# Making the scores of two attention steps together in a fused attention and mixture-of-experts kernel

## The chip, the cores and the metric

One NeuronCore of a Trainium2 chip runs the whole kernel. The metric is the device time of one execution in microseconds (us). Nothing runs on the other cores.

## The reference

The input is x (4 batches, 2048 tokens, 256 features, float32). The reference is one transformer layer, with a layer norm behind each half:

```python
Q = sign(x * sign(bv_q)); K = sign(x * sign(bv_k)); V = x * sign(bv_v)
scores = einsum('btd,bsd->bts', Q, K) * d ** -0.5
attn = where(causal, sigmoid(scores * 4.0), 0.0)
x = layernorm(x + einsum('bts,bsd->btd', attn, V))

# top-1 mixture of 32 experts, capacity 320 rows each
probs = softmax(x @ w_router); top1 = argmax(probs)
y = (silu(buf @ w_gate) * (buf @ w_up)) @ w_down   # per expert
out = layernorm(x + where(accepted, y[slot] * gate, 0.0))
```

The attention has no softmax: each weight is a sigmoid of its own score, so a block of weights can be used as soon as its scores exist.

## The kernel before

The kernel is written with an instruction stream for each engine by hand; semaphores order them. Five engines work: TensorE (PE), VectorE (DVE), ScalarE (ACT), GpSimd (POOL), and SyncE (SP), which only issues DMAs. Each engine runs its own stream in order.

**Attention steps.** A batch has four groups of 512 queries (g = 0 to 3). Group g needs 4g + 4 blocks of 128 keys, so a batch has 4 + 8 + 12 + 16 = 40 steps (`NS`), numbered k = 0 to 39; the groups begin at k = 0, 4, 12 and 24. There are four batches, 160 steps in all. A step goes through three engines:

- `scores(b, k)` on PE: two bfloat16 matmuls (line 899) of 128 keys by up to 512 queries into one of four PSUM banks (`SB = 4`, bank k % 4). The last four steps of a group lie on the diagonal: they have 512, 384, 256 and 128 queries, and one small matmul more for the mask (line 896).
- `weights(b, k)` on ACT: two sigmoids of the same scores, one rounded into `hl_ring` (line 694), one in full back into the bank (line 696).
- `low(b, k)` on DVE: their difference, the low part of the weight (line 1173). It frees the bank.
- `values(b, k)` on PE: for each tile of 128 queries three matmuls of 256 columns (lines 921 to 923), so 12 in a full step and 12, 9, 6 and 3 on the diagonal. They add up in PSUM over the steps of the group.

`scores` of step n waits until `low` of step n - 4 has freed the bank (semaphore `al_ready`). `values(b, k)` waits for `low(b, k)` too. PE's order in every step k from 2 on is: the scores of step k + 4, then the values of step k.

**Work between the steps.** Behind the values of chosen steps PE does work for the groups that are finished: `turn_x1` (8 transposes, line 940), `router` (16 matmuls of 32 output rows, line 953), `turn_logits` (line 959) and `counts` (5 small bfloat16 matmuls, lines 966 to 971). The steps are written out in tables; a key is the group, and group 3 is done in the batch that follows:

```python
TURN = {3: 5, 0: 11, 1: 20, 2: 29}
ROUTE = {3: 6, 0: 12, 1: 24, 2: 30}
LTURN = {3: 6, 0: 13, 1: 26, 2: 31}
COUNT = {3: 8, 0: 17, 1: 28, 2: 34}
NORM = {3: (6, 6, 7, 7), 0: (10, 11, 11, 11), 1: (21, 22, 23, 23), 2: (30, 31, 31, 32)}   # ACT
COPY = {3: 9, 0: 14, 1: 23, 2: 33}     # ACT
LCOPY = {3: 9, 0: 16, 1: 28, 2: 34}    # ACT
```

ACT's tables count ACT's own steps: `normalise` (line 704) stands behind `weights` of the steps in `NORM`, `copy_x1t` (two copies, line 711) behind `weights` of the step in `COPY`, and so on. `turn_x1` waits for the four normalised tiles, the copies wait for `turn_x1`, each half of `router` waits for one of the two copies, `copy_lgt` (line 716) waits for `router`, and `turn_logits` waits for `copy_lgt`. ACT is thus several steps ahead of PE in step numbers: the copies that PE's step 6 waits for stand behind `weights` of step 9, and those that its step 30 waits for behind `weights` of step 33.

DVE adds the residual from PSUM at the end of a group (line 1180), takes statistics, and makes the routing decisions. SP waits at line 347 for a count of `scores_ready` before it transposes the signs of the next batch by DMA (line 348).

After the attention comes the expert part (from about 313 us): `gate_up` (lines 1077 to 1085) and `down` (lines 1100 to 1111). The change doesn't touch it.

Of the kernel before, what the change touches and what calls it, by code (L numbers as in the profile page):

```python
# [34 lines left out]
SB = 4  # L35
# [28 lines left out]
def bass_postln_attn_moe_kernel(nc, x, bv_q, bv_k, bv_v, w_router, w_gate, w_up, w_down, out):  # L64
# [16 lines left out]
    NS = len(STEPS)  # L81
# [8 lines left out]
    with ExitStack() as ctx:  # L90
# [168 lines left out]
        def atleast(eng, s, value, settle=False):  # L259

            if isinstance(value, int) and value <= 0:
                return
            if settle and not isinstance(value, int):
                value = eng.to_reg(value)
                eng.wait_ge(consts, 11)
            eng.wait_ge(s, value)
# [43 lines left out]
        def cols(k):  # L312

            g, j = STEPS[k]
            return g, j, max(0, j - GT * g) * P
# [553 lines left out]
        def _(pe):  # L869
# [8 lines left out]
            def scores(b, k):  # L878

                g, j, lo = cols(k)  # L880
                n = b * NS + k
                if j == 0:
                    if b == 0:
                        pe.wait_ge(qt_ready, g + 1)
                    else:
                        pe.wait_ge(qt_in, 16 * ((b - 1) * NG + g + 1))
                if j == GT * g:
                    if n == 0:
                        pe.wait_ge(key_first, 1)
                    pe.wait_ge(kt_ready, DC * (b * NG + g + 1) - 1)  # L890
                atleast(pe, al_ready, n - SB + 1)
                o = ps[:, k % SB, lo:GQ]
                diag = j >= GT * g
                if diag:

                    mm(ps[:, k % SB, lo:lo + P], identb[:, :], maskb[:, :], start=True, stop=False,
                       skip_group_check=True)
                for c in range(DC):
                    last = mm(o, k_t[:, c, j * P:(j + 1) * P], q_t[:, g, c, lo:GQ],  # L899
                              start=(c == 0 and not diag), stop=(c == DC - 1), skip_group_check=diag)  # L900
                last.then_inc(scores_ready, 1)

            def values(b, k):

                g, j, lo = cols(k)
                n = b * NS + k
                r = k % WRING
                if n == 0:
                    pe.wait_ge(v_first, 1)
                elif n == 1 or j == GT * g:  # L910
                    pe.wait_ge(v_ready, b * NG + g + 1)
                pe.wait_ge(ah_ready, n + 1)
                pe.wait_ge(al_ready, n + 1)
                for i in range(lo // P, GT):
                    if j == 0 and i % 2 == 0:

                        atleast(pe, res_ready, (b * NG + g - 1) * GT + i + 2)
                    o = ps[:, PV + i // 2, (i % 2) * D:(i % 2 + 1) * D]
                    ah = hl_ring[:, 0, r, i * P:(i + 1) * P]
                    al = hl_ring[:, 1, r, i * P:(i + 1) * P]  # L920
                    mm(o, ah, v_hl[:, 0, j, :], start=(j == 0 and i % 2 == 0), stop=False, skip_group_check=True)  # L921
                    mm(o, ah, v_hl[:, 1, j, :], start=False, stop=False, skip_group_check=True)  # L922
                    last = mm(o, al, v_hl[:, 0, j, :], start=False, stop=(j == GT * g + i), skip_group_check=True)  # L923
                last.then_inc(pv_done, 1)

            def turn_signs(b, q):
                n = b * NG + q
                pe.wait_ge(sgn_ready, n + 1)
                o = ps[:, M1, :].bitcast(BF16).rearrange("p (c t) -> p c t", c=DC)
                for c in range(DC):  # L930
                    for i in range(GT):
                        last = nc.tensor.transpose(o[:, c, i * P:(i + 1) * P], sgn[:, c, i, :],
                                                   identb[:, :])
                last.then_inc(sgn_turned, 1)

            def turn_x1(G, par):
                for i in range(GT):
                    pe.wait_ge(x1_ready, G * GT + i + 1)
                    for c in range(DC):
                        last = nc.tensor.transpose(ps[:, M0 + c, i * P:(i + 1) * P],  # L940
                                                   xrow[:, par, i, c * P:(c + 1) * P], ident[:, :])
                last.then_inc(x1_turned, 1)

            def router(G):
                if G == 0:
                    pe.wait_ge(w_r_in, 16)
                for c in range(DC):
                    if G == B * NG - 1 and c == 1:
                        pe.wait_ge(x1t_late, 1)
                    else:  # L950
                        pe.wait_ge(x1t_ready, DC * G + c + 1)
                    for i in range(GT):
                        last = mm(ps[i * E:(i + 1) * E, M0, 0:P], w_r[:, c, :], x1_t[:, c, i * P:(i + 1) * P],  # L953
                                  start=(c == 0), stop=(c == DC - 1))
                last.then_inc(lgt_done, 1)

            def turn_logits(G):
                pe.wait_ge(lgt_ready, G + 1)
                nc.tensor.transpose(ps[:, M0, 0:GT * E], lg_t[:, :], ident[:, :]).then_inc(logits_done, 1)

            def counts(G):

                pe.wait_ge(hot_ready, G + 1)
                pe.wait_ge(seen_ready, G + 1)
                rows = hot[:, G % 2, :, :]
                mm(logits, tri[:, :], rows[:, 0:GT, :], start=True, stop=False, skip_group_check=True)
                for h in range(GT - 1):
                    mm(logits[:, h + 1:GT, :], onesb[:, :],
                       rows[:, h, :].unsqueeze(1).broadcast_to([P, GT - 1 - h, E]), start=False, stop=False,
                       skip_group_check=True)  # L970
                mm(logits, onesb[:, :], rows[:, GT, :].unsqueeze(1).broadcast_to([P, GT, E]), start=False, stop=True,
                   skip_group_check=True).then_inc(counts_done, 1)

            def batch(b, first, last):
                for k in range(NS):
                    if first and k < 2:
                        values(0, k)
                        if k == 0:
                            turn_signs(0, 1)
                        else:  # L980
                            scores(0, SB)
                            scores(0, SB + 1)
                    else:
                        if k + SB < NS:
                            scores(b, k + SB)
                        elif not last:
                            scores(b + 1, k + SB - NS)
                        values(b, k)
                    for g in (3, 0, 1, 2):
                        if g == 3 and first:  # L990
                            continue
                        G = (b - 1 if g == 3 else b) * NG + g
                        if k == TURN[g]:


                            prepared = NG if b > 0 else 2 + sum(PREP[q] < k for q in (2, 3))
                            atleast(pe, slot_ready, G)
                            pe.wait_ge(qt_ready, prepared)
                            turn_x1(G, g % 2)
                        if k == ROUTE[g]:  # L1000
                            router(G)
                        if k == LTURN[g]:
                            turn_logits(G)
                        if k == COUNT[g]:
                            counts(G)
                    for q in range(NG):
                        if first and k == PREP[q] and q not in AHEAD:
                            pe.wait_ge(qt_ready, q)
                            turn_signs(0, q)
# [5 lines left out]
            for k in range(SB):  # L1015
                scores(0, k)
            keep_warm(5, bank=M0)
            batch(0, True, False)
            for b in range(1, B - 1):
                batch(b, False, False)  # L1020
            batch(B - 1, False, True)
            G = B * NG - 1
            pe.wait_ge(al_ready, B * NS)
# [475 lines left out]
```

## Time and profile before

| what | value |
|---|---|
| median of 3 runs | 538.89 us (538.89 to 539.34) |
| profiled execution | 538.01 us |
| its span, first to last instruction | 536.3 us |
| PE busy | 515.2 us, 96% of the span |
| DVE, ACT, POOL busy | 406.3, 380.8, 384.6 us |
| attention steps on PE | to 301 us |

The span is what the trace shows; the 1.7 us between it and the time of the profiled execution lie ahead of the first and behind the last instruction. Matmuls are pipelined, so their busy times overlap: a matmul's row shows its start and how long it was in the array, and two that follow each other without a gap start less than one duration apart. What a group of matmuls costs is read as the distance between the end of the row ahead of it and its own end.

### The profile page before, as it was taken

What the parts mean: (1) busy time and instruction counts of PE and PEld (TensorE: products, weight loads), DVE (VectorE), ACT (ScalarE), POOL (GpSimd) and SP (SyncE); (2) the same over time, 40 slices, a digit from 0 to 9 for tenths busy, and PEclk for the clock granted to TensorE, in tenths of its full rate; (3) what the DMA queues carried; (4) which work ended last, traced back from release to release, by engine and by line L of the source; (5) the groups of instructions that cost most, each with busy time, mean ns of one, the idle gap of its engine ahead of it and who ended that gap; (6) DMA issues with size and microseconds to landing.
All of it is one profiled execution on the core that took longest, in us unless ns stands there. A gap on an engine that the chain in (4) does not pass through costs nothing.

```text
span 536.3 us, 12197 instructions
## 1 busy us (share of the span) xinstructions
PE 515.2 (96%) x4028; PEld 457.9 (85%) x4028; DVE 406.3 (76%) x1026; ACT 380.8 (71%) x775; POOL 384.6 (72%) x497
## 2 busy tenths in 40 slices
PE   6999999999999999999999999999999999999992
PEld 5889899898998898998989648999889999999981
DVE  3785787876777948788766636888888888888873
ACT  5885969769878869788686414777677677776762
POOL 4547877777879678777785270578877878787876
PEclk9999999999999999999999999999999999999997
DMA  7995332263332533328841016487776667786211
GB/s 247 371 355 195 90 99 61 79 178 101 110 85 81 108 117 87 95 46 275 247 156 62 1 49 153 125 252 208 224 207 193 199 202 213 216 241 184 76 41 51
DMA packets 91903, 81.54 MB, mean 152 GB/s; under 512 B 31626, under 2 KB 83066, under 8 KB 91840
## 3 DMA queue, kind: packets, MB, share of 16 engines
q1 hardware_dynamic: 84848, 66.39, 42.5%
q0 software_dynamic: 6912, 14.30, 7.9%
q8 instruction: 33, 0.54, 0.4%
q14 instruction: 30, 0.25, 0.2%
q10 hardware_dynamic: 80, 0.07, 0.0%
HBM read 44.33 MB, written 37.90 MB: 153 GB/s over the span
## 4 chain that ended last, share of the span: by engine, by line
PE 91%; POOL 2%; issue 2%; DVE 2%; DMA 2%; ACT 1%; SPq 0%; ACTq 0%; POOLq 0%; DVEq 0%
PE ps L921 12%; PE ps L922 12%; PE ps L923 12%; PE ps L899 11%; PE ps L1077 8%; PE ps L1085 7%; PE ps L1078 7%; PE ps L1103 5%; PE ps L1111 3%; PE ps L1050 3%; PE ps L940 2%; PE ps L953 2%; PE ps L1100 1%; PE ps L1102 1%; PE ps L1101 1%
## 5 line engine op out<-in xcount | busy, mean ns | idle before, releaser
L921 PE MATMUL ps<-v_hl,hl_ring 128*128 128x256 f32 x544 | 178.6, 328 | 0.3 <-DVE hl_ring L1173 0.3
L922 PE MATMUL ps<-v_hl,hl_ring 128*128 128x256 f32 x544 | 153.6, 282 | 0.0
L923 PE MATMUL ps<-v_hl,hl_ring 128*128 128x256 f32 x544 | 153.3, 282 | 0.0
L921 PEld LDWEIGHTS ps<-v_hl,hl_ring 128*128 128x128 f32 x544 | 103.5, 190 | 15.1 <-issue 0.7
L1173 DVE TENSOR_TENSOR hl_ring<-ps,hl_ring 128x512 fp32r<-128x512 f32 (+3 forms) x160 | 94.1, 602 | 19.0 <-ACT ps L696 14.0
L922 PEld LDWEIGHTS ps<-v_hl,hl_ring 128*128 128x128 f32 x544 | 103.8, 191 | 2.7
L923 PEld LDWEIGHTS ps<-v_hl,hl_ring 128*128 128x128 f32 x544 | 103.4, 190 | 0.0
L694 ACT ACTIVATE hl_ring<-ps 128x512 fp32r<-128x512 f32 (+3 forms) x160 | 86.3, 539 | 22.2 <-PE ps L899 21.9
L696 ACT ACTIVATE ps<-ps 128x512 f32<-128x512 f32 (+3 forms) x160 | 87.4, 546 | 0.0
L536 POOL DMA_INDIRECT expert_rows<-xrow,slot x64 | 64.3, 1005 | 29.0 <-issue 22.8
L899 PE MATMUL ps<-q_t,k_t 128*128 128x512 bf16 (+3 forms) x320 | 85.1, 350 | 0.0
L1077 PE MATMUL ps<-hl_ring,v_hl 128*128 128x320 f32 x256 | 80.8, 328 | 0.3 <-DVE hl_ring L1441 0.3
L1078 PE MATMUL ps<-hl_ring,v_hl 128*128 128x320 f32 x256 | 76.0, 309 | 0.0
L620 POOL DMA_INDIRECT out_dram<-alone,ids x55 | 56.9, 1035 | 16.6 <-issue 14.4
L1077 PEld LDWEIGHTS ps<-hl_ring,v_hl 128*128 128x128 f32 x256 | 48.1, 188 | 7.0 <-issue 6.5
L1279 DVE TENSOR_TENSOR v_hl<-xall,v_hl 128x1280 fp32r<-128x1280 f32 x32 | 47.8, 1497 | 7.1 <-issue 7.1
L816 ACT ACTIVATE a_buf<-ps 128x320 f32<-128x320 f32 x64 | 28.0, 437 | 34.0 <-PE ps L1085 34.0
L1078 PEld LDWEIGHTS ps<-hl_ring,v_hl 128*128 128x128 f32 x256 | 48.2, 188 | 0.4
L1085 PE MATMUL ps<-hl_ring,v_hl 128*128 128x320 f32 x256 | 48.0, 310 | 0.0
L489 POOL TENSOR_TENSOR v_hl<-z,v_hl 128x1024 fp32r<-128x1024 f32 x15 | 36.0, 2402 | 12.7 <-ACT v_hl L686 12.7
L732 ACT ACTIVATE v_hl<-xall 128x1280 fp32r<-128x1280 f32 x32 | 40.5, 1266 | 1.6 <-PE ps L923 1.6
L834 ACT ACTIVATE alone<-z,zrs 128x256 f32<-128x256 f32 x54 | 29.0, 594 | 17.7 <-POOL zrs L607 16.3
(163 smaller groups left out, 1127.0 us busy)
## 6 DMA issues: line engine op xcount, KB each, us to landing
expert_rows<-xs SPq DMA_DIRECT2D x40, 258.0 KB, 6.2
xs<-expert_rows SPq DMA_DIRECT2D x32, 258.0 KB, 2.8
xall<-in_L_attn_x_dram SPq DMA_DIRECT2D x16, 512.0 KB, 5.1
out_dram<-alone SPq DMA_DIRECT2D x16, 512.0 KB, 3.5
xall<-in_L_ffn_w_gate_dram SPq DMA_DIRECT2D x32, 256.0 KB, 3.9
xall<-in_L_ffn_w_up_dram SPq DMA_DIRECT2D x32, 256.0 KB, 4.3
xall<-in_L_ffn_w_down_dram SPq DMA_DIRECT2D x32, 256.0 KB, 4.8
xs<-expert_rows SPq DMA_DIRECT2D x31, 64.5 KB, 3.1
```

The lines of the kernel that those rows point to most:

```text
L536: g_.indirect_dma_start(out=buf_rows, out_offset=bass.IndirectOffsetOnAxis(ap=slot[:, par, i:i + 1], axis=0), in_=xrow[:, par, i, :], in_o ...
L620: g_.indirect_dma_start(out=out_rows, out_offset=bass.IndirectOffsetOnAxis(ap=ids[:, e % NIDS, t:t + 1], axis=0), in_=o_s[e % 3][:, t, :], ...
L694: s_.activation(hl_ring[:, 0, k % WRING, lo:GQ], ps[:, k % SB, lo:GQ], ACT.Sigmoid, scale=0.25)\
L696: s_.activation(ps[:, k % SB, lo:GQ], ps[:, k % SB, lo:GQ], ACT.Sigmoid, scale=0.25)\
L899: last = mm(o, k_t[:, c, j * P:(j + 1) * P], q_t[:, g, c, lo:GQ], start=(c == 0 and not diag), stop=(c == DC - 1), skip_group_check=diag)
L921: mm(o, ah, v_hl[:, 0, j, :], start=(j == 0 and i % 2 == 0), stop=False, skip_group_check=True)
L922: mm(o, ah, v_hl[:, 1, j, :], start=False, stop=False, skip_group_check=True)
L923: last = mm(o, al, v_hl[:, 0, j, :], start=False, stop=(j == GT * g + i), skip_group_check=True)
L1077: mm(o, wh, xh[:, c, :], start=(c == 0), stop=False)
L1078: mm(o, wl, xh[:, c, :], start=False, stop=False)
L1085: last = mm(o, wh, xl[:, c, :], start=False, stop=(c == DC - 1))
L1173: v_.tensor_tensor(hl_ring[:, 1, r, lo:GQ], ps[:, k % SB, lo:GQ], hl_ring[:, 0, r, lo:GQ].bitcast(F32), ALU.subtract).then_inc(al_ready, 1)
```

## The change

In every even step PE makes the scores of steps k + 3 and k + 4, then the values of step k. In odd steps it makes only values. Step 1 of the first batch makes the scores of step 4 and leaves those of step 5 to step 2. No instruction is added or removed, and the other engines' streams are as they were. Since `NS` is even, the scores of even steps stay where they were (ahead of the values of the step four before), and those of odd steps go behind the values of the step four before, and behind whatever PE does after these values.

```diff
                         else:
                             scores(0, SB)
-                            scores(0, SB + 1)
                     else:
-                        if k + SB < NS:
-                            scores(b, k + SB)
-                        elif not last:
-                            scores(b + 1, k + SB - NS)
+
+                        for n in (k + SB - 1, k + SB) if k % 2 == 0 else ():
+                            if n < NS:
+                                scores(b, n)
+                            elif not last:
+                                scores(b + 1, n - NS)
                         values(b, k)
```

## Rows read from the trace of the kernel before

**Rows 1.** The page: busy times, and the clock granted to PE in 40 slices.

```profile
PE 515.2 (96%) x4028; PEld 457.9 (85%) x4028; DVE 406.3 (76%) x1026; ACT 380.8 (71%) x775; POOL 384.6 (72%) x497
...
PEclk9999999999999999999999999999999999999997
```

**Rows 2.** Busy times by stretch: PE, PEld, DVE, ACT, POOL, clock, DMA, GB/s.

```profile
13.00:301.00 288.00, 286.77 (x2472) 258.86 (x2472) 216.83 (x575) 227.80 (x484) 211.65 (x251) 1.00 0.47 140
```

**Rows 3.** Waits of PE and of its weight loads, 13 to 301 us, in full.

```profile
PE ps L959 <- ACT lg_t L716: 1.2, 3, 0.4
...
PEld ps L899 <- issue: 2.2, 11, 0.2
PEld ps L959 <- ACT lg_t L716: 2.0, 3, 0.7
PEld ps L921 <- ACT hl_ring L694: 0.3, 1, 0.3
PEld ps L921 <- DVE res L1180: 0.2, 1, 0.2
PEld ps L899 <- DVE hl_ring L1173: 0.2, 1, 0.2
```

**Rows 4.** PE's timeline around two score blocks: start, duration, instructions.

```profile
120.55 0.28 PE L923 MATMUL ps<-v_hl,hl_ring 128*128 128x256 f32 x1
120.67 0.61 PE L899 MATMUL ps<-q_t,k_t 128*128 128x512 bf16 x2
...
122.55 1.03 PE L940 MATMUL ps<-ident,xrow 128*128 128x128 f32 x8
123.42 0.59 PE L899 MATMUL ps<-q_t,k_t 128*128 128x512 bf16 x2
123.66 0.47 PE L921 MATMUL ps<-v_hl,hl_ring 128*128 128x256 f32 x1
```

**Rows 5.** The same timeline where 128-query scores stand ahead of values.

```profile
97.05 0.28 PE L899 MATMUL ps<-q_t,k_t 128*128 128x128 bf16 x2
97.14 0.37 PE L921 MATMUL ps<-v_hl,hl_ring 128*128 128x256 f32 x1
```

**Rows 6.** The same timeline behind a router.

```profile
142.21 0.65 PE L953 MATMUL ps<-x_t,w_r 128*32 128x128 f32 x16
142.79 0.60 PE L899 MATMUL ps<-q_t,k_t 128*128 128x512 bf16 x2
```

**Rows 7.** The same timeline in the expert part, half-width output ahead of full.

```profile
401.60 0.60 PE L1111 MATMUL ps<-xall,act_h 128*64 128x256 f32 x4
402.13 0.42 PE L1077 MATMUL ps<-hl_ring,v_hl 128*128 128x320 f32 x1
402.39 0.31 PE L1078 MATMUL ps<-hl_ring,v_hl 128*128 128x320 f32 x1
```

**Rows 8.** Groups of weight loads, 30 to 250 us: busy time, mean ns.

```profile
L922 PEld LDWEIGHTS ps<-v_hl,hl_ring 128*128 128x128 f32 x410 | 78.2, 191 | 2.1
...
L899 PEld LDWEIGHTS ps<-q_t,k_t 128*128 128x128 bf16 x242 | 17.2, 98 | 3.9 <-issue 1.8
```

**Rows 9.** Timelines of ACT and of PE, batch 1, steps 5 and 6 of PE.

```profile
93.02 0.48 ACT L694 ACTIVATE hl_ring<-ps 128x384 fp32r<-128x384 f32 x1
93.39 0.48 ACT L696 ACTIVATE ps<-ps 128x384 f32<-128x384 f32 x1
94.19 1.09 ACT L711 ACTIVATE x_t<-ps 128x512 f32<-128x512 f32 x2 [0.32 <-PE ps L940]
...
93.12 1.03 PE L940 MATMUL ps<-ident,xrow 128*128 128x128 f32 x8
95.79 0.64 PE L953 MATMUL ps<-x_t,w_r 128*32 128x128 f32 x16
```

**Rows 10.** Timelines of ACT and of PE, batch 1, steps 29 and 30 of PE.

```profile
138.15 0.60 ACT L694 ACTIVATE hl_ring<-ps 128x512 fp32r<-128x512 f32 x1
138.64 0.59 ACT L696 ACTIVATE ps<-ps 128x512 f32<-128x512 f32 x1
140.46 1.08 ACT L711 ACTIVATE x_t<-ps 128x512 f32<-128x512 f32 x2 [1.22 <-PE ps L940]
...
139.38 1.03 PE L940 MATMUL ps<-ident,xrow 128*128 128x128 f32 x8
```

**Rows 11.** Waits for scores: the SP queue's own, and ACT's from 30 to 250 us.

```profile
SPq L347 <- PE ps L899: 7.8, 3, 3.4
...
ACT hl_ring L694 <- PE ps L899: 16.7, 26, 1.2
```

## The prediction

> **What bounds the kernel now.** I read the page first, then the stretches, then PE's waits, then PE's timeline matmul by matmul. The page shows PE busy for 515.2 us of a span of 536.3 us, at full clock in all but the last slice [rows 1]. The stretch of the attention steps says it more sharply: from 13 to 301 us PE is busy 286.77 of 288 us, DVE 216.83, ACT 227.80 and POOL 211.65 us [rows 2]. A busy PE could still be one with slow matmuls, so the waits must be read as well: in these 288 us PE waits for another engine only at line 959 (3 times) and its weight loads three times more for 0.2 to 0.3 us [rows 3]. Nobody is late anywhere else. So the attention is as long as PE's stream of matmuls with the seams between them, and a change of PE's order can do two things only: change what the seams cost, or make another engine late where it is not late now. Behind 301 us nothing changes, and what PE loses or gains before then moves the end one for one.
>
> **The seams: how often each kind occurs.** PE's order follows from the loop and the four tables, so the seams can be counted by writing out the order of blocks for 4 x 40 steps, before and after. Each block of scores that follows values directly: 96 before, 55 after (41 fewer), because the second block of each pair now follows scores. Values behind 128-query scores: 15 before, 1 after (14 fewer), because the 128-query steps are odd (3, 11, 23, 39) and now have the next step's scores behind them. What comes instead: `router` stands in even steps, so behind 12 of the 15 routers now come values where scores came (the other three are followed by line 959 as before). `counts` is followed by values 11 times where it never was; `turn_x1` 4 times and `turn_logits` 7 times.
>
> **What each kind costs.** Costs are distances from end to end.
>
> - Scores behind values: from the end of line 923 at 120.83 to the end of both score matmuls at 121.28 is 0.45 us. Behind the transposes it is 123.58 to 124.01, 0.43 us [rows 4]. So the change from values to scores costs 0.02 us. 41 fewer: -0.8 us.
> - Values behind scores: the first value matmul ends 0.12 us after scores of 512 queries (124.01 to 124.13) [rows 4], the same as between value matmuls. Behind scores of 128 queries it is 97.33 to 97.51, 0.18 us [rows 5]; a row is only good to 0.01 us, and I take 0.05 us more than the ordinary 0.12. 14 fewer: -0.7 us. The reason is in the weight loads: that of a value matmul takes 191 ns, that of a score matmul 98 ns [rows 8], and behind a short matmul the long load shows.
> - Behind a router: the scores end 0.53 us after it (142.86 to 143.39) [rows 6] where 0.43 is ordinary, so 0.10 us are lost now. Values behind a router are nowhere in this trace. The bounds: at least 0.10 us as for scores, which would change nothing; the nearest row for more is in the expert part, where a full-width matmul with the same kind of 32-bit weights follows half-width ones: it ends 0.35 us after them (402.20 to 402.55), its successor 0.15 us later [rows 7], so 0.20 us lost. I take 0.20, since the load that can't be hidden there is of the long kind. 12 x (0.20 - 0.10) = +1.2 us; between 0 and +1.2.
> - Behind `counts`, whose last matmul is a short bfloat16 one like the 128-query scores: between 0 and 0.05 us by rows 5, I take 0.05. 11 times: +0.6 us.
> - Behind `turn_x1` and `turn_logits`: 11 times between 0 and 0.05 us. Their matmuls are longer, I take 0; at most +0.5 us.
>
> The seams together: -1.5 + 1.2 + 0.6 = +0.3 us, between -1.5 and +0.8 us.
>
> The Trainium skill ("TensorE: Matmul & The Clock Gate", section LDWEIGHTS) gives the weight load a time that depends on the number of columns alone. By that rule values behind a router would cost what scores do there, and the sum of the seams would be 1.2 us lower. The trace doesn't agree with it: for the same 128 columns it has 191 and 98 ns.
>
> **When the scores come, and who waits for them.** The scores of even steps stay in the same place of PE's work. Those of odd steps n are made behind the values of step n - 4 and not ahead of them, so they are up to 1.4 us later (12 x 0.12), and by the 1.03 us of `turn_x1` more where that stands in between (steps 5, 11 and 29, all odd). PE's own demand is unchanged: `low` of step k is needed at the same point of PE's work as before, by the scores ahead of `values(k)` or by these values themselves. And values of odd steps end one score block (0.43 us) earlier, which helps the residual adds that read them. The added lag is hidden as long as `weights` and `low` have that much to spare. That PE waited for `low` only once, 0.2 us, in 288 us [rows 3] says that they have some; ACT itself waits for scores 26 times between 30 and 250 us, 16.7 us in all [rows 11], so it mostly catches up at once. SP's wait for a count of scores ends up to 1.4 us later; it had waited 7.8 us in three places [rows 11]. Behind it stand the sign transpose and the next load of x, both for steps of the next batch, so this costs nothing.
>
> Two places have no such slack: the routers of group 3 (PE's step 6) and of group 2 (step 30), because the copies that they wait for stand on ACT behind `weights` of an odd step, 9 and 33, made just then.
>
> - Step 6, batch 1 [rows 9]. Before: `weights(9)` starts at 93.02 and ends at 93.87, the copies run from 94.19, and the router starts at 95.79. After: the values of step 5 end 0.40 us earlier (the three-tile scores of step 9 went), `turn_x1` ends at 94.15 - 0.40 = 93.75, the scores of step 9 at 94.13. `weights(9)` runs from 94.17 to 95.02; the copies, which overlap it by 0.1 us, end at 94.92 + 1.09 = 96.01. PE asks for the second copy about 0.13 us into the router, at 95.92 (an estimate: a fifth of its 0.64 us, since most of these are the emptying of its last matmuls). It waits 0.1 us. Three batches: 0.4 us.
> - Step 30 [rows 6, 10]. `turn_x1` ends at 140.41 - 0.45 = 139.96, the scores of step 33 at 140.41 (before, `weights(33)` had begun at 138.15), `weights(33)` runs to 140.45 + 1.08 = 141.53, the copies end at 141.43 + 1.08 = 142.51. PE asks for it at 142.21 + 0.13 = 142.34: it waits 0.2 us. Four batches: 0.8 us.
>
> Together +1.2 us. Below this, nothing, if the copies come a little sooner; above, each place may lose 0.5 us if ACT is also held by late normalisations: 3.5 us.
>
> **The sum.** +0.3 + 1.2 = +1.5 us on 538.01 us of the profiled execution: 539.5 us. The median of the runs lies 0.9 us above that execution, so I expect a median of 538.9 + 1.5 = 540.4 us.
>
> **Rivals.**
>
> 1. *No router waits, and values behind a router cost what scores do.* Then only the savings and the small costs stay: -1.5 + 0.6 = -0.9 us, 538.0 us; with nothing behind `counts` either, 537.4 us. For it: the waits that I found are 0.1 and 0.2 us, and rows 7 are of another stage. It is the one on the other side, and only with both conditions does it pass 0.2%. It decides if the second copy ends before PE is at the router's second half.
> 2. *ACT is late by more than one place.* The later scores of step 31 push its normalisations to where `turn_x1` of step 29 needs them, and `weights(33)` waits in turn. Each place then costs some 0.5 us: 7 x 0.5 - 1.5 + 1.8 = +3.8 us, 542.7 us. For it: four activations (two of weights, two of norms or copies, 0.5 us apart) are queued between. Against it: ACT is busy only 79% of the stretch.
> 3. *The seams cancel and the waits are half as large*: within 1 us of before, 539 to 539.9 us. All of the terms are small, so this is the neighbour of my forecast.
> 4. *Each seam costs far more than a row shows*, and halving their number is a real gain: 41 x 0.05 or so, -2 us, 536.9 us. Against it: rows 4 leave no room for it.
>
> **How the numbers follow.** My forecast (a loss between 1.1 and 3 us) has 0.41; rival 2 0.09; rival 3, with the weaker forms of rival 1, 0.38; rival 1 in full 0.08; rival 4 0.04. A difference of 0.2% (1.1 us) is about what a measurement of this kernel can tell from no change. That gives slower 0.50, the same 0.38, faster 0.12. The range goes from 538.0 us to 542.5 us; its ends come from rivals 1 and 2. The single number is 540.2 us, the sum rounded down a little because the largest seam term is an upper bound.
>
> **What the profile would show.** The lines of PE's waits should have new entries, line 953 waiting for line 711, seven times in the attention, 0.1 to 0.3 us each; line 959 should wait three times as before. In the timeline pairs of score blocks should end 0.86 us apart from the values ahead of them plus 0.02, and values behind a router 0.3 us behind it. `weights` of odd steps should start later, those of even steps mostly unchanged. The prediction is wrong if PE has waits at line 921 or 899 for line 1173 or 694 (then the lag was not hidden), if no wait at line 953 shows, or if values behind a router end only 0.2 us behind it.

## The result, and the profile after

| | before | changed |
|---|---|---|
| median | 538.89 us (6 runs) | 543.80 us (6 runs, 542.79 to 544.02) |
| profiled execution, span | 538.01, 536.3 us | 543.86, 541.4 us |
| ratio | | 1.0085, 95% interval 1.0075 to 1.0095 |

The changed kernel is slower: its median lies 4.9 us (0.9%) above that of the kernel before, and the measured ratio of the runs, which need not be the quotient of the two medians here and below, is 1.0085. I had forecast 540.2 us, slower, with a range to 542.5 us: the sign was right, the forecast loss of 1.3 us was about a quarter of what came, and the measured time lies outside my range. In the changed kernel and in those of the experiments the lines from the edit on are one to four further down: `low` is line 1174, the residual add 1181, the gate multiply 1247 (before: 1173, 1180 and 1246).

First the page of the changed kernel [rows 1 are its partners before].

```profile
PE 518.7 (96%) x4028; PEld 454.3 (84%) x4028; DVE 413.4 (76%) x1026; ACT 380.4 (70%) x775; POOL 384.1 (71%) x497
...
PEclk9999999999999999999999999999999999999996
```

PE's busy share is unchanged and says nothing: the clock is the same, and the waits are short. The stretches (columns as in [rows 2]) place the loss: with a boundary at 306 us in place of 301, the part behind it has the same 235 us, and PE is busy for 220.87 us of it where it was 220.75. The first row is of the kernel before, the other two of the changed one.

```profile
301.00:536.00 235.00, 220.75 (x1489) 192.71 (x1487) 184.79 (x444) 145.94 (x279) 167.41 (x223) 0.99 0.55 162
...
13.00:306.00 293.00, 290.09 (x2470) 255.17 (x2469) 223.75 (x575) 227.33 (x484) 211.07 (x251) 1.00 0.45 138
306.00:541.00 235.00, 220.87 (x1490) 192.73 (x1488) 184.93 (x444) 145.95 (x279) 167.45 (x223) 0.98 0.55 162
```

So the loss lies in the attention. PE's waits and those of its weight loads there, to be held against [rows 3]:

```profile
PE ps L921 <- DVE xs L1181: 1.7, 3, 0.6
PE ps L959 <- ACT lg_t L716: 1.2, 3, 0.4
...
PEld ps L921 <- issue: 2.8, 12, 0.3
PEld ps L921 <- DVE xs L1181: 2.3, 3, 0.8
PEld ps L959 <- ACT lg_t L716: 2.0, 3, 0.7
PEld ps L953 <- ACT x_t L711: 1.4, 7, 0.2
PEld ps L921 <- ACT hl_ring L694: 0.9, 4, 0.3
PEld ps L899 <- DVE hl_ring L1174: 0.9, 3, 0.3
PEld ps L940 <- ACT xrow L704: 0.3, 1, 0.3
```

Each row gives the total, the number of waits and the longest. The seven waits of the router for its copies are there as forecast. The largest entry is one that I had not thought of: three times a value matmul waits for the residual add. PE's timeline shows where (batch 1; the same in batches 2 and 3): inside the values of step 0.

```profile
84.32 0.71 PE L899 MATMUL ps<-q_t,k_t 128*128 128x128 bf16 x4
84.90 0.36 PE L921 MATMUL ps<-v_hl,hl_ring 128*128 128x256 f32 x1
...
85.57 0.28 PE L923 MATMUL ps<-v_hl,hl_ring 128*128 128x256 f32 x1
86.40 0.39 PE L921 MATMUL ps<-v_hl,hl_ring 128*128 128x256 f32 x1 [0.55 <-DVE xs L1181]
```

From the end of line 923 (85.85) to the end of the next line 921 (86.79) it is 0.94 us where 0.12 is ordinary: 0.82 us lost. The first value matmul of the step, at 84.90, also ends 0.23 us behind its scores, 0.11 more than ordinary; its weight load began at 84.87, 0.12 us after the first residual add had ended (84.75). Together 0.93 us, three times: 2.8 us, more than half of the loss.

The values of step 0 open a new group. They overwrite the PSUM banks that group 3 of the batch before has filled, so tiles 0 and 1 wait for the first residual add, and tiles 2 and 3 for the second, which DVE makes behind `low` of step 1. Why that add is late can be followed backwards through four engines. The same stations in the changed kernel (ACT, DVE, POOL, ACT, ACT, DVE):

```profile
76.14 0.49 ACT L694 ACTIVATE hl_ring<-ps 128x384 fp32r<-128x384 f32 x1 [1.27 <-PE ps L899]
...
77.11 0.56 DVE L1174 TENSOR_TENSOR hl_ring<-ps,hl_ring 128x384 fp32r<-128x384 f32 x1 [1.28 <-ACT hl_ring L694]
77.58 0.94 DVE L1245 RECIPROCAL quot<-sg 128x128 f32<-128x128 f32 x1
78.56 0.29 DVE L1247 SCALAR_TENSOR_TENSOR quot<-quot,sg 128x128 f32<-128x128 f32 x1
...
78.93 2.38 POOL L482 TENSOR_TENSOR z<-xall,bv_row 128x1024 f32<-128x1024 f32 x1 [1.39 <-DVE quot L1247]
...
81.34 1.06 ACT L686 ACTIVATE v_hl<-z 128x1024 fp32r<-128x1024 f32 x1 [1.18 <-POOL z L482]
...
84.25 0.48 ACT L694 ACTIVATE hl_ring<-ps 128x384 fp32r<-128x384 f32 x1
...
85.66 0.68 DVE L1181 TENSOR_TENSOR xs<-ps,xall 128x512 f32<-128x512 f32 x1
```

and in the kernel before:

```profile
74.21 0.49 ACT L694 ACTIVATE hl_ring<-ps 128x384 fp32r<-128x384 f32 x1 [0.17 <-PE ps L899]
...
76.15 0.94 DVE L1244 RECIPROCAL quot<-sg 128x128 f32<-128x128 f32 x1
77.13 0.29 DVE L1246 SCALAR_TENSOR_TENSOR quot<-quot,sg 128x128 f32<-128x128 f32 x1
...
77.50 2.39 POOL L482 TENSOR_TENSOR z<-xall,bv_row 128x1024 f32<-128x1024 f32 x1 [0.57 <-DVE quot L1246]
...
79.92 1.06 ACT L686 ACTIVATE v_hl<-z 128x1024 fp32r<-128x1024 f32 x1 [1.73 <-POOL z L482]
...
82.82 0.48 ACT L694 ACTIVATE hl_ring<-ps 128x384 fp32r<-128x384 f32 x1
...
84.29 0.69 DVE L1180 TENSOR_TENSOR xs<-ps,xall 128x512 f32<-128x512 f32 x1
```

Each row of the first list minus its partner in the second gives the lateness as it travels. `weights` of step 37 has +1.93 us: 1.44 us because its scores are odd and came behind the values of step 33, and 0.5 us because PE's whole stream was already that late at step 32. Then come the gate's reciprocal and multiply, which stand on DVE behind `low` of step 37, +1.43, GpSimd's signed values of the next batch, for which an explicit wait makes it wait for that multiply, +1.43, the high values on ACT +1.42, `weights` of step 1 behind them on ACT +1.43, the second residual add +1.37. The step from 1.93 to 1.43 us is slack on DVE: before, it had work without a pause up to `low` of step 37, and now it is idle for 1.28 us ahead of it.

Before, there was next to no slack at the end of the chain: the add was done at 84.98, and the first matmul of tile 2 began at 85.19, its weight load at 85.07.

```profile
85.07 0.19 PEld L921 LDWEIGHTS ps<-v_hl,hl_ring 128*128 128x128 f32 x1
85.19 0.28 PE L921 MATMUL ps<-v_hl,hl_ring 128*128 128x256 f32 x1
```

In the changed kernel PE came to the values of step 0 about 0.5 us later anyway, by its own lateness. So of the 1.37 us of the add only some 0.9 us were new to PE, and these it lost in full.

### The profile page after: what moved, and what is told of

Same layout as the page of the kernel before. It is cut to its first block, busy times and chain, and to the rows that moved or that the text cites. A ratio compares the mean times of both kernels' runs of the same rounds, so it can differ in the third digit from the quotient of the medians.

```text
span 541.4 us, 12197 instructions
## 1 busy us (share of the span) xinstructions
PE 518.7 (96%) x4028; PEld 454.3 (84%) x4028; DVE 413.4 (76%) x1026; ACT 380.4 (70%) x775; POOL 384.1 (71%) x497
## 4 chain that ended last, share of the span: by engine, by line
PE 88%; issue 3%; POOL 3%; DVE 2%; ACT 2%; DMA 1%; ACTq 0%; POOLq 0%; DVEq 0%; SPq 0%
PE ps L921 12%; PE ps L922 11%; PE ps L923 11%; PE ps L899 10%; PE ps L1078 8%; PE ps L1086 7%; PE ps L1079 7%; PE ps L1104 5%; PE ps L1112 3%; PE ps L1051 3%; PE ps L940 2%; PE ps L953 2%; PE ps L1101 1%; PE ps L1103 1%; PE ps L1102 1%
## 5 line engine op out<-in xcount | busy, mean ns | idle before, releaser
L921 PE MATMUL ps<-v_hl,hl_ring 128*128 128x256 f32 x544 | 169.5, 312 | 1.9 <-DVE xs L1181 1.7
L922 PE MATMUL ps<-v_hl,hl_ring 128*128 128x256 f32 x544 | 153.4, 282 | 0.0
L923 PE MATMUL ps<-v_hl,hl_ring 128*128 128x256 f32 x544 | 153.2, 282 | 0.0
L1174 DVE TENSOR_TENSOR hl_ring<-ps,hl_ring 128x512 fp32r<-128x512 f32 (+3 forms) x160 | 95.5, 603 | 34.6 <-ACT ps L696 20.7
L899 PE MATMUL ps<-q_t,k_t 128*128 128x512 bf16 (+3 forms) x320 | 73.9, 348 | 0.0
```

Source lines behind the costliest of these rows:

```text
L1174: v_.tensor_tensor(hl_ring[:, 1, r, lo:GQ], ps[:, k % SB, lo:GQ], hl_ring[:, 0, r, lo:GQ].bitcast(F32), ALU.subtract).then_inc(al_ready, 1)
```

## The experiments

The scores that go late are made a table in most of them, so that any set of steps can be moved. With all odd steps in `LATE` the order is that of the changed kernel, with none that of the kernel before:

```diff
-                        for n in (k + SB - 1, k + SB) if k % 2 == 0 else ():
+                        for n in [m for m in (k + SB - 1, k + SB) if (m % NS in LATE) == (m == k + SB - 1)]:
```

The medians of the kernel before beside the experiments were 539.14 us for `e1` to `e4` and 538.95 us for the others, and 538.89 us beside the changed kernel. What an experiment gives or takes is told below by the bare medians; against the kernel before beside each, it can differ by 0.3 us.

The profiles allow a finer reading than the medians. PE does the same matmuls in every kernel, so the end of the last value matmul of a step can be compared with its partner in the kernel before. At even steps (odd ones for `e6` and `e11`) the scores that stand ahead are the same in both orders, and what the difference gains from one such step to the next is lost there. I call it PE's lag.

**One step put back.** `e1_undo37`:

```diff
+LATE = tuple(n for n in range(1, 40, 2) if n != 37)
```

> The changed kernel, but the scores of step 37 of every batch are put back ahead of the values of step 33. Theory A (a chain from step 37: late scores hold its weights on ScalarE, these its low part on VectorE, that the gate multiply behind it, that GpSimd's signed values of the next batch, these the high values on ScalarE and with them the weights of steps 0 and 1 and the second residual add, for which the values of step 0 wait): the 0.8 us gap inside the values of step 0 of batches 1 to 3 goes, about 2.6 us less than the changed kernel, 541.2 us. Theory B (ScalarE is late at the start of a batch because all odd steps come late, above all 39): the gap stays within 0.2 us, 543.5 us. Theory C (the loss is in the seams of TensorE's stream): within 0.1 us of the changed kernel.

Measured: 540.95 us, 1.0031 (1.0019 to 1.0043) of before. 2.9 us of the loss are gone with one step of forty. Theory A stands; B and C expected no such fall. At step 0 of batches 1 to 3 PE's lag grows by 0.87, 0.86 and 0.85 us in the changed kernel and falls by 0.07 us each time here. PE's own waits in the attention, in full (those of its weight loads not counted):

```profile
PE ps L960 <- ACT lg_t L717: 1.2, 3, 0.4
```

**The wait on GpSimd taken away.** `e2_no_pace`:

```diff
-                    pool.wait_ge(gate_step, 3 * (n + 2) + 2)
                     values_signed(b + 1, 1)
```

> The changed kernel without GpSimd's wait for the gate multiply ahead of the signed values of the next batch's second quarter (a wait that only sets the time, since no operand depends on it). Theory A: GpSimd starts these values about 1.4 us earlier, the high values on ScalarE no longer come late, and the gap in step 0 goes: 541.2 us or a little less, unless the two engines then slow each other at the gate multiply. Theory B: ScalarE is as late as before, 543.8 us. Theory C: 543.8 us.

Measured: 541.72 us, 1.0036 (1.0024 to 1.0048) of before. The scores are as late as in the changed kernel; only GpSimd no longer waits. At the start of batches 1 to 3 the lag falls by 0.07 us as in `e1_undo37`, so the whole gap is gone. That the median gives 2.1 us back and not 2.8 us fits another place: behind the values of step 20 of batch 1 the transposes wait for a normalised tile, and the lag grows by 0.71 us there.

**One step moved alone.** `e3_only37`, from the kernel before:

```diff
+LATE = (37,)
```

> The kernel before with one edit: the scores of step 37 alone go behind the values of step 33, beside those of step 38. Theory A: the whole chain is there with one late step, the gap of 0.8 us comes back in batches 1 to 3, about 2.6 us more than before, 541.5 us. Theory B: one late step does little, within 0.3 us of before, 539 us. Theory C: 538.9 us.

Measured: 541.64 us, 1.0041 (1.0027 to 1.0055) of before. The gap is back in step 0, with the same releaser, and PE's timeline is otherwise that of the kernel before: its lag grows by 0.85, 0.85 and 0.84 us at step 0 of batches 1 to 3, and behind the first values of batch 0 by no more than 0.03 us anywhere else.

```profile
85.36 0.28 PE L924 MATMUL ps<-v_hl,hl_ring 128*128 128x256 f32 x1
86.20 0.39 PE L922 MATMUL ps<-v_hl,hl_ring 128*128 128x256 f32 x1 [0.56 <-DVE xs L1184]
```

**The gate one step earlier.** `e12_gate36` keeps every late score and the wait on GpSimd:

```diff
-GATE = {3: (14, 15), 0: (18, 19), 1: (30, 30), 2: (37, 39)}
+GATE = {3: (14, 15), 0: (18, 19), 1: (30, 30), 2: (36, 39)}
```

> The changed kernel with the first part of group 2's gate on VectorE behind the low part of step 36 in place of step 37. Theory A: the gate, and GpSimd behind it, no longer wait for the late scores of step 37, so the gap at the start of batches 1 to 3 goes though all scores are as late as in the changed kernel: 541.2 us. Theory B: no change, 543.8 us.

Measured: 541.71 us, 1.0051 (1.0038 to 1.0064) of before. GpSimd starts its signed values at 77.78 in place of 78.93 and waits 0.24 us for the multiply:

```profile
77.78 2.38 POOL L483 TENSOR_TENSOR z<-xall,bv_row 128x1024 f32<-128x1024 f32 x1 [0.24 <-DVE quot L1250]
```

With these four the chain is cut at three different links (scores, DVE's queue, GpSimd's wait) and built up alone once, and each gives or takes 2.1 to 2.9 us by the medians. In all three that cut it, the lag falls by 0.07 us at the start of each of batches 1 to 3 where it grew by 0.86: 2.8 us.

**The control for the wait.** `e8_before_no_pace` takes the same line out of the kernel before.

> The kernel before without GpSimd's wait for the gate multiply. The control for the run of the changed kernel without it: theory A says that the wait is hidden in the kernel before (0.5 us to spare at the value tiles of step 0), so within 0.5 us of before, 538.9 us; if the removal itself is a gain of 2 us here too, that run proves nothing.

Measured: 539.10 us, 1.0002 (0.9994 to 1.0011). The wait costs nothing there, and behind the first values of batch 0 PE's lag stays at 0.41 us to the end, so the gain in `e2_no_pace` is the chain's. The 0.5 us to spare of my expectation was misread: by the rows above, it is 0.1 to 0.2 us.

**The routers' steps put back.** `e4_undo_routers`:

```diff
+LATE = tuple(n for n in range(1, 40, 2) if n not in (9, 31, 33))
```

> The changed kernel, but the scores of steps 9, 31 and 33 are put back to their places before. Theory A with its second part (the copies behind weights 9 and 33 and the normalised tiles behind weights 31 are what the router and the transposes wait for): the waits at these places go, 4 times 0.3 us and 3 times 0.1 us, so 1.3 to 1.6 us less than the changed kernel, 542.3 us; the gap at the start of a batch stays. Rival: these waits are set by TensorE's own transposes and not by the late scores: 543.8 us.

Measured: 542.39 us, 1.0058 (1.0044 to 1.0072), 1.4 us less than the changed kernel. The waits of the router for line 711 no longer appear among PE's and its weight loads' waits; the gap in step 0 stays.

**Both put back.** `e5_undo_all4` has 9, 31, 33 and 37 on time.

> The changed kernel with the scores of steps 9, 31, 33 and 37 put back. Theory A: both kinds of waits are gone and only the changed seams are left: 12 routers with values behind them at 0.09 us more, counts with values behind them, against some 35 fewer changes from values to scores at 0.02 us and 11 fewer 128-query scores ahead of values at 0.05 us: within 0.7 us of before, 539.4 us. Theory C (the seams cost more than the rows show): more than 1 us above before.

Measured: 540.32 us, 1.0024 (1.0015 to 1.0033), 1.4 us above before. That lies above my 0.7 us, and just into what theory C expected. PE's lag accounts for 1.1 of the 1.3 us by which its profiled span is longer. 0.16 us are there at the first values of batch 0, ahead of every moved block, and differ between executions (0.41 us in `e8_before_no_pace`). At step 31 of batch 0, and less in batch 1, the values start late because of `low`, 0.3 us in all. The transposes of batch 3 wait for a normalised tile behind the values of step 20, 0.3 us. A wait of the kernel before, at step 24 of batch 1, is gone, -0.3 us. What is left, 0.65 us in small steps behind the routers and between scores and values, is the seams, where my rows gave 0.3 us.

**Even steps late in place of odd ones.** `e6_even_late`, and `e11_even_cover`, which has the scores of steps 4, 8, 16 and 28 on time:

```diff
+LATE = tuple(range(0, 40, 2))                                          # e6
+LATE = tuple(n for n in range(0, 40, 2) if n not in (4, 8, 16, 28))    # e11
```

> The kernel before with the pairs made in odd steps: the scores of even steps are late and those of odd steps stay. Theory A: step 37 comes in time, so the chain at the batch's end has no late member, and the copies behind weights 9 and 33 come in time too; routers have scores behind them again. No gap in step 0, some waits possible at step 24, whose low part had 0.4 us to spare, and whose copies stand behind step 23: between 538.5 and 541 us, 539.5 us. Theory B (late scores as such cost, whichever): as the changed kernel, 543 us or more.

> The kernel with the scores of even steps late, but those of steps 4, 8, 16 and 28 of every batch on time, so that the values that open a group (steps 0, 4, 12 and 24) have scores ahead of them again. Theory D: in the kernel with even steps late these values waited for the residual add that has to read their banks first, 10 times, since the 0.43 us of scores that hid it were gone; here the waits go and it comes down from 544.8 us to about 541.5 us. Rival: the low parts of late even steps are what is late: 544 us or more.

Measured: `e6_even_late` 544.78 us, 1.0116 (1.0101 to 1.0130); `e11_even_cover` 540.76 us, 1.0040 (1.0026 to 1.0055). The first was forecast badly: the worst of all, though it has no late step 37. Its weight loads waited for residual adds ten times:

```profile
PEld ps L922 <- DVE res L1184: 2.7, 7, 0.7
...
PEld ps L922 <- DVE xs L1184: 1.9, 3, 0.6
```

In the kernel before, a block of scores stands ahead of the values that open a group, and its 0.43 us are the time in which DVE reads the banks. `e11_even_cover` puts these blocks back and gains 4.0 us, though the other even steps are as late as in `e6_even_late`; of the waits for a residual add it has 0.7 us left, most of them these:

```profile
PEld ps L922 <- DVE xs L1184: 0.5, 3, 0.2
```

Why it stays 1.8 us above the kernel before shows in its profile too: the transposes wait for a normalised tile, 2.0 us by the weight loads, and most of PE's lag (0.73, 0.99 and 0.40 us in batches 1 to 3) grows behind the values of step 20.

**Only 128-query scores late.** `e7_diag`, from the kernel before:

```diff
+LATE = (3, 11, 23, 39)
```

> The kernel before with only the 128-query scores of steps 3, 11, 23 and 39 moved behind the values of the step four before, beside the next step's scores. By the rows, 14 times 0.05 us for the weight load behind them and 14 times 0.02 us for the change from values to scores are saved: 0.9 us less than before, 538.0 us, since none of these steps is in the chain of step 37. Theory B: at least one of them (39 above all) makes ScalarE late: slower than before.

Measured: 539.42 us, 1.0010 (0.9996 to 1.0024). No gain. In the profile other places take back more than the seams save: its weight loads wait for `low` (1.1 us, 3 times), for a normalised tile (0.8 us, 3 times) and for a residual add (0.4 us, once). These places make 1.7 us of PE's lag; without them and the start it would be 0.4 us ahead, not the 0.9 us of my rows. The profiled execution took 541.06 us, 1.6 us above the median, so a usual one has less of these waits.

**A wait of the kernel before.** `e9_logits_late` separates router and logit transpose of group 3, and `e10_late_3_11` adds `LATE = (3, 11)`:

```diff
-LTURN = {3: 6, 0: 13, 1: 26, 2: 31}
+LTURN = {3: 7, 0: 13, 1: 26, 2: 31}
-COUNT = {3: 8, 0: 17, 1: 28, 2: 34}
+COUNT = {3: 9, 0: 17, 1: 28, 2: 34}
```

> The kernel before with the order of scores untouched, and group 3's logit transpose put behind the values of step 7 in place of step 6, its counts behind step 9 in place of 8. TensorE waited 0.62 us three times between router and logit transpose in one and the same step. With a step between them this should go: 1.8 us less than before, 537.1 us. Rival: VectorE's routing for group 3 comes a step later and holds the low parts of steps 10 and 11, so that half or all of it is lost again: 538 to 539 us.

> The same as the kernel with the later logit transpose, and the scores of steps 3 and 11 late (pairs 3 and 4, 11 and 12), the two 128-query steps that no transpose, router or batch end waits for. If the seam costs hold, 8 times 0.07 us less: 0.5 us less than that kernel, 536.6 us. If late scores cost something at any place: no gain or slower.

Measured: 538.61 us, 0.9992 (0.9979 to 1.0005), and 538.85 us, 1.0000 (0.9991 to 1.0008). The wait at line 959 is gone from the list of PE's waits, and PE is 0.53 us earlier behind it in each of batches 1 to 3, but 0.31 us of that are lost again by step 12. Neither can be told from the kernel before, and no version beats it.

## Why the prediction was wrong

- **Where the time is lost: right.** Only the attention changed, PE's stream sets its length, and it moved the end one for one.
- **The seams: right, within 0.4 us.** Behind a router the first value matmul ends 0.31 us after it (changed kernel, 70.20 to 70.51), 0.2 more than ordinary as the expert part's [rows 7] had said. The rule of the Trainium skill ("TensorE: Matmul & The Clock Gate", section LDWEIGHTS), by which a weight load's time depends on its columns alone, is again not what the trace shows: value matmuls lose 0.2 us behind a router where score matmuls lost 0.1 us. For all seams I had 0.3 us, and `e5_undo_all4` has about 0.65.

```profile
69.39 0.81 PE L953 MATMUL ps<-x_t,w_r 128*32 128x128 f32 x16
...
70.12 0.39 PE L921 MATMUL ps<-v_hl,hl_ring 128*128 128x256 f32 x1
```

- **The routers' waits: right in place and number, and in size.** Seven waits, 1.4 us in all by the weight loads (0.17 us at step 6, 0.22 us at step 30); I had 1.2 us. In the row above the router is in the array for 0.81 us, before 0.65 [rows 6]. What I left out of the sum is its neighbour: I had let `turn_x1` of step 29 run without a wait, though its last normalised tile stands behind `weights(32)` on ACT (only rival 2 has it late). It takes 1.01 us from the last value matmul (66.15) to its end, 0.87 before:

```profile
65.87 0.28 PE L923 MATMUL ps<-v_hl,hl_ring 128*128 128x256 f32 x1
66.07 1.09 PE L940 MATMUL ps<-ident,xrow 128*128 128x128 f32 x8
```

With steps 9, 31 and 33 on time (`e4_undo_routers`) PE's lag no longer grows there.

- **The step that failed: "The added lag is hidden as long as `weights` and `low` have that much to spare."** I looked for the lag only at `low` and at the copies, that is at what PE waits for from the step itself. Two things were left out. DVE's stream has other work queued behind `low`: the gate multiply behind that of step 37, for which GpSimd waits. I had not looked at GpSimd, since none of its instructions moved. And values that open a group wait not only for their `low` but for the residual add, which stands behind `low` of an odd step, 1. I used the residual adds only for a gain ("values of odd steps end one score block earlier"). This wait was at nothing in my sum. It measured 2.8 us in the trace, and 2.1 to 2.9 us by the four experiments.
- **My own sign of it.** I had called the prediction wrong if PE waited at line 921 or 899 for line 1173 or 694. It does: seven such waits of its weight loads, 1.8 us, where the kernel before had two of 0.3 and 0.2 us. They say rightly that the lag wasn't hidden, but they aren't where the time went: the three of line 899 come at step 2 of batches 1 to 3, right behind the gap, and PE's lag doesn't grow there (1.33 us at step 0 and 1.32 us at step 2 of batch 1).
- **The rivals.** Rival 2 had a right mechanism (late scores pile up in ACT's queue) for the smaller part of the loss and gave 542.7 us; none named the start of a batch. Rivals 1, 3 and 4 are out: the loss is 4.9 us, and no seam became cheap enough to matter.
- **The sum, set right:** seams +0.3, routers +1.4, transposes of step 29 0.14 x 4 = +0.6, start of batches 1 to 3 +2.8: +5.1 us, against 4.9 us measured and 5.1 us between the spans. That it closes so well is partly luck: the seams are rather more than I had, and two terms that it leaves out (+0.4 and -0.3 us) nearly cancel. PE's lag says where the time went without any model: it is 5.15 us at the end of the attention. 2.6 us of it grew at the start of batches 1 to 3 (the 2.8 us, less the 0.07 us that is saved there each time), 1.8 us between steps 28 and 32 of the four batches (transposes, router wait and router seam), 0.4 us behind the values of step 20 in batch 3, where the transposes wait for a normalised tile, -0.3 us at step 24 of batch 1, where a wait of the kernel before is gone, and 0.7 us elsewhere, mostly behind the other routers.

## What to carry to other kernels

When an instruction is moved later, list what is queued behind its consumers on each engine in order, and follow each of these to its own waiters, across engines whose code was not touched; the slack to use is the smallest on any of those paths. A block of work ahead of a buffer's reuse can be cover for the reader of that buffer: before moving it, ask who reads in that time. A wait that only paces an engine ties two schedules together, and moving such a station by one step (`e12_gate36`, 2.1 us) can be worth nearly as much as putting the moved block back (`e1_undo37`, 2.9 us).

## What the runs showed of the hardware that was not expected

The gate multiply on VectorE has the same shape each time, 15 times in a run, and most take 0.29 to 0.47 us. Three took 1.31 to 1.38 us in the kernel before; in the changed one three took 1.32 to 1.33 us and four 1.86 to 1.87 us. Each long one began 0.18 to 0.73 us after an operation on GpSimd had begun and ended 0.14 to 0.15 us after that had ended. This is most of the rise of VectorE's busy time from 406.3 to 413.4 us without one instruction more: the 15 multiplies sum to 8.2 us before and 13.7 us in the changed kernel. The changed kernel, DVE and POOL:

```profile
141.19 1.86 DVE L1247 SCALAR_TENSOR_TENSOR quot<-quot,sg 128x128 f32<-128x128 f32 x1
...
141.00 1.90 POOL L520 TENSOR_TENSOR alone<-xrow,small 128x1024 f32<-128x1024 f32 x1
```

The kernel before has 139.92 with 1.38 us (to 141.30) beside 139.26 with 1.90 us (to 141.16) on GpSimd:

```profile
139.92 1.38 DVE L1246 SCALAR_TENSOR_TENSOR quot<-quot,sg 128x128 f32<-128x128 f32 x1
...
139.26 1.90 POOL L520 TENSOR_TENSOR alone<-xrow,small 128x1024 f32<-128x1024 f32 x1
```

So this multiply did not run slower beside GpSimd, it waited for the end. The Trainium skill says so ("SBUF — State Buffer", in the row on the shared port pair of its table of terms): the pair is held for a full instruction, and the loser is blocked. Not every VectorE instruction is held: beside GpSimd's 2.38 us from 78.93 in the changed kernel, the ten on VectorE, the 128x256 `low` among them, took their usual 0.15 to 0.42 us.

For a change of order this means that a shift of a few tenths of a microsecond can add up to the length of a GpSimd operation to a short VectorE one. In `e7_diag` it reached PE. In batch 1 the multiply of step 30 took 2.03 us, `low` of step 31 stood behind it, and the next scores waited 0.31 us:

```profile
140.42 2.03 DVE L1250 SCALAR_TENSOR_TENSOR quot<-quot,sg 128x128 f32<-128x128 f32 x1
...
143.66 0.60 PE L900 MATMUL ps<-q_t,k_t 128*128 128x512 bf16 x2 [0.31 <-DVE hl_ring L1177]
```

PE's lag grew by 0.37 us there, by 0.18 us in batch 0, where the multiply took 1.84 us, and not at all in batches 2 and 3, where it took 0.44 and 0.43 us. In `e4_undo_routers` it grew by 0.35, 0.35, 0.10 and 0.10 us there (0.1 us of each is the router's seam), with multiplies of 1.85, 1.85, 1.46 and 0.51 us. So this is part of why the small gains of `e7_diag` did not appear; its other waits are of other kinds, and no run changes the multiply's place alone.
